# Loading each expert's first weights as 512 pieces of 2 KB in place of 128 pieces of 8 KB

## The reference, cut to what matters

```
logits = xf @ wr + br
topk_vals, topk_idx = jax.lax.top_k(logits, K)          # E = 4 experts, K = 2
h = jax.nn.gelu(jnp.einsum('nd,edh->enh', xf, w1) + b1[:, None, :], approximate=False)
y = jnp.einsum('enh,ehd->end', h, w2) + b2[:, None, :]
```

## Time and profile before

| | |
|---|---|
| Median of 3 runs | 2584.3 us (2577.14 to 2584.51) |
| Profiled execution | 2576.5 us, its span 2574.7 us |
| PE (TensorE) busy | 2089.3 us, 81% of the span |
| DVE, ACT, POOL busy | 1759.0, 1570.7, 1016.1 us |
| DMA | 375.69 MB in 306117 packets, mean 146 GB/s |
| Queue q1 (SP's issues) | 38.6% of 16 engines' span |
| Queue q0 (POOL's) | 8.9% |
| Loads of `moe_w_tile` | 94 of 1024 KB, median 5.3 us from issue to landing |

### The profile page before, as it was taken

The page is one execution under the profiler, slowest core; times in us unless marked ns, Lnnn a source line. Parts: engine busy times, 40 slices in busy tenths (PEclk is TensorE's granted clock), DMA queues, the critical chain, the costliest instruction groups (busy, mean ns, idle before and its releaser), DMA issues. The chain is left out here.

```text
span 2574.7 us, 46905 instructions
## 1 busy us (share of the span) xinstructions
PE 2089.3 (81%) x12000; PEld 1628.2 (63%) x12000; DVE 1759.0 (68%) x7891; ACT 1570.7 (61%) x2744; POOL 1016.1 (39%) x1092
## 2 busy tenths in 40 slices
PE   1344688788888888898898889999888998999965
PEld 1122466676766666676676767777766787777742
DVE  4777667676777777677787778787767554544343
ACT  1034446456666776676677677777666676666542
POOL 1445455545444544344455444444444212111110
PEclk8655699898999999999999899999989999999976
DMA  7354534344445555534555455555554445455431
GB/s 268 98 149 119 172 117 145 111 141 136 127 129 165 170 150 145 170 112 131 150 177 156 141 147 159 175 165 150 143 177 136 142 129 168 136 160 169 150 99 51
DMA packets 306117, 375.69 MB, mean 146 GB/s; under 512 B 127122, under 2 KB 251447, under 8 KB 292924
## 3 DMA queue, kind: packets, MB, share of 16 engines
q1 hardware_dynamic: 274848, 297.02, 38.6%
q0 software_dynamic: 28672, 68.21, 8.9%
q10 hardware_dynamic: 2332, 7.47, 0.7%
HBM read 291.23 MB, written 72.93 MB: 141 GB/s over the span
## 5 line engine op out<-in xcount | busy, mean ns | idle before, releaser
L1204 POOL DMA_INDIRECT w_win<-in_windows,w_idx x512 | 542.0, 1059 | 831.3 <-DMA w_win<-in_windows,w_idx 665.4
L1595 PE MATMUL bank<-moe_w,moe_hidden_T 128*128 x2528 | 640.3, 394 | 13.5 <-DVE moe_y L1037 11.5
L1579 PE MATMUL bank<-moe_xT,moe_w_tile 128*128 128x256 f32 (+1 forms) x3008 | 641.3, 358 | 8.4 <-ACT moe_xT L1364 8.3
L1579 PEld LDWEIGHTS bank<-moe_xT,moe_w_tile 128*128 128x128 f32 x3008 | 517.7, 197 | 85.2 <-ACT moe_xT L1364 14.5
L1595 PEld LDWEIGHTS bank<-moe_w,moe_hidden_T 128*128 128x128 f32 x2528 | 475.6, 197 | 88.8 <-issue 26.7
L818 DVE TENSOR_TENSOR w_prod<-w_win,w_hat 128x36 f32<-128x36 f32 x4096 | 494.3, 218 | 27.2 <-DMA w_win<-in_windows,w_idx 24.1
L1381 ACT ACTIVATE moe_hidden_T<-bank,moe_b 128x256 f32<-128x256 f32 (+1 forms) x752 | 288.8, 437 | 210.7 <-PE bank L1579 207.5
L1238 POOL DMA_INDIRECT moe_y_back<-moe_out_sorted,rows_back x128 | 129.4, 1011 | 275.9 <-DMA moe_y_back<-moe_out_sorted,rows_back 157.3
L1224 POOL DMA_INDIRECT moe_in_sorted<-c,rows x128 | 141.9, 1109 | 236.4 <-DMA moe_in_sorted<-c,rows 100.5
L1381 ACT ACT_TABLE_LOAD x129 | 165.5, 1283 | 72.9 <-PE bank L1579 70.6
L1123 DVE SCALAR_TENSOR_TENSOR hidden_back<-bank,back_stats,hidden_back 128x512 f32<-128x512 f32 x128 | 95.5, 746 | 115.9 <-ACT hidden_back L1421 115.5
(11 more groups left out here) (258 smaller groups left out, 3797.7 us busy)
## 6 DMA issues: line engine op xcount, KB each, us to landing
moe_w_tile<-in_moe_w SPq DMA_DIRECT2D x94, 1024.0 KB, 5.3
L_cond_W<-in_L_cond_W SPq DMA_DIRECT2D x128, 256.0 KB
adapters<-in_adapter SPq DMA_DIRECT2D x128, 192.5 KB
gamma_beta<-in_gamma_beta SPq DMA_DIRECT2D x128, 128.0 KB
moe_x<-moe_in_sorted SPq DMA_DIRECT2D x64, 256.0 KB
moe_out_sorted<-moe_y SPq DMA_DIRECT2D x64, 256.0 KB
x_front<-in_x SPq DMA_DIRECT2D x32, 256.0 KB
w_win<-in_windows,w_idx POOLq DMA_INDIRECT x512
```

The costliest lines, as they stand in the source:

```text
L1204: gp.indirect_dma_start(out=V[:, g_ * WLEN:(g_ + 1) * WLEN], out_offset=None, in_=t["windows"], in_offset=bass.IndirectOffsetOnAxis(ap=idx ...
L1579: last = te.matmul((H0, H1)[r % 2][:, (f % FPU) * TILE:(f % FPU) * TILE + width(n)], W1[n % 3][:, d * F + f * P:d * F + (f + 1) * P], XT[: ...
L1595: last = te.matmul(Y[:, u * D:(u + 1) * D], hT[:, (f % (2 * FPU)) * TILE + u * P:(f % (2 * FPU)) * TILE + (u + 1) * P], ap(moe2, weight + ...
```

## The change

The host lays the experts' first weights out in another order, and the load reads them in that order. Before, each partition's 8 KB (2048 values) of an expert lay in one piece. Now the 2048 values are cut in four parts of 512 values (2 KB, `WPK`); part 0 of all 128 partitions comes first, then part 1, and so on. An expert is then 1 MB in one piece, made of four stretches of 256 KB. The load reads 4 pieces of 2 KB for each partition, 256 KB apart, and puts them in the same places in the buffer as before. The register that holds the plan's offset is used as a row number in an array with 128 values a row, so the same number still points at the expert.

```
+WPK = 512
...
-                sp.dma_start(W1[n % 3][:, :], t["moe_w1"][:, bass.ds(col, NDB * F)]).then_inc(s_w1[n % 3], 16)
+                sp.dma_start(W1[n % 3][:, :].rearrange("p (c f) -> p c f", f=WPK),
+                             t["moe_w1"][bass.ds(col, NDB * F), :].rearrange("(c p k) d -> p c (k d)", p=P, k=WPK // P)
+                             ).then_inc(s_w1[n % 3], 16)
...
-        "moe_w1": np.concatenate([blocks(w) for w in a["L1_ffn_w1"]], 1),
+        "moe_w1": np.concatenate([blocks(w).reshape(P, -1, WPK).transpose(1, 0, 2).reshape(-1, P) for w in a["L1_ffn_w1"]], 0),
```

## The result

The changed kernel takes 2590.02 us in the median of 20 runs (2571.62 to 2607.24), the kernel before 2579.36 us (2562.62 to 2590.18, 20 runs). The ratio is 1.0044, with a 95% interval of 1.0023 to 1.0065: slower by 11 us, where 3 us were forecast. Two later comparisons, each on another chip, gave 1.0087 (1.0052 to 1.0121) and 1.0094 (1.0059 to 1.0128). A ratio here is that of the comparison with its runs; it isn't always the quotient of the two medians (for the last it would be 1.0070).

A forecast was written before the change was run, and what follows sets the result against it. TensorE was taken to bound the stretch of the loads, not the DMA engines. A tenth of POOL's and SP's delays, 2.1 + 1.3 = 3.4 us, on the median 2584.3 gave 2587 us, range 2578 to 2595 (over all cases 2571 to 2603).

The forecast's parts named there:

- Nobody waits for a load: Expert-weight loads: issued about 46 us ahead and landing after 5.3 us, so a load's own speed is worth nothing.
- The transfer itself: DMA engines: a load in 2 KB pieces takes 2.68 us an engine, not 2.47; 20 us more for 94 loads.
- A tenth of the delays reaches the end: POOL and SP delays: 2.1 us of 20 us and 1.3 us of 12 us lengthen the run, 3.4 us together.
- SP's issue: SP issuing a load: 0.47 us for 512 pieces, 0.13 us more a load, 12 us of SP in all.
- The gathers beside a load: POOL's gathers: each waits for the whole load as before, 0.21 us longer, 20 us of POOL's time.
- Rival 1: POOL's gathers get in after 8 pieces, held 0.67 us instead of 2.41; faster, 2567 us; chance 0.12.
- Rival 2: SP's issues behind a load stand until its pieces drain, 1.2 us a load; slower, 2599 us; chance 0.18.
- Rival 3: Load still made in 8 KB packets, or the 0.21 us vanishes in idle DMA time; 2584 us; chance 0.08.

The follow-up runs named there:

- the cut alone: Kernel before with 512 pieces of 2 KB a load, each partition's kept in its own row, 4 KB apart: ratios 1.0007 and 0.9981 against the kernel before.
- The doubled transfer: Kernel before with each load followed by a copy of the same 1 MB into DRAM: 2703.05 against 2574.82 us, ratio 1.0488.
- the finer cut: Kernel before with 2048 pieces of 512 bytes a load, each partition's in its own row, 1 KB apart: 2570.10 against 2581.67 us, ratio 0.9953.
- the order alone: Kernel before with only the DRAM order changed, each expert 1 MB in one piece, still read in 128 pieces of 8 KB: ratio 1.0015.

## Why the prediction was right and where it was wrong

The time fell within the range and moved to the side that the sum gave, and there was luck in it: the sum came out at 3 us for 11 us, and 2590 us lies near 2587 us partly because the kernel before came out at 2579 us over 20 runs, 5 us below the median that the sum started from. Most of the chance, 0.66, lay on a time within 0.3%, and all three comparisons put the change above that (0.44, 0.87 and 0.94%). The third has 2599.72 us, outside the forecast's own 2578 to 2595 us.

- **"Nobody waits for a load":** right. No run shows a wait of TensorE for one.
- **"The transfer itself", 0.21 us more a load:** right as a sum, and by luck. Inside a load the packets take 0.084 us as read (199 packets, 104.7%), but over whole loads they take 0.099 us in the cut alone and 0.104 us in the change, and those of 8 KB 0.388 us and not 0.309 us. A load's packets went from 3.10 to 3.32 us an engine, 0.22 us more, of which the cut is 0.08 us and the order 0.14 us. The prediction gave all of it to the cut; that a partition's pieces now lie 256 KB apart was costed at nothing, and no sentence says so.
- **"A tenth of the delays reaches the end":** this is the step that failed. The order's 13 us of DMA time cost 20 us (2599.72 against 2579.93 us), more than its whole. The doubled transfer's 233 us cost 128 us. The cut's own 8 us cost nothing that can be told (0.9981 and 1.0007), and the finer cut's 49 us came with a gain. There is no one share. The sum also has 2.1 and 1.3 us as tenths of 20 and 12 us, where they are 2.0 and 1.2 us.
- **"SP's issue", 0.13 us:** too much; 0.04 us, and 0.388 us even for 2048 pieces. Some 0.86 us of other work for SP ahead of each load cost nothing at all.
- **"The gathers beside a load" wait for the whole of it:** right. Take the window gathers that are issued with a load (from 0.2 us ahead of it to 1.5 us behind) and for which the next gather waits: in two profiles of the kernel before 42 of 44 had their last packet behind the load's last, and in three of the change 66 of 67. From the load's issue to the next gather it is 5.85 and 5.93 us in the median before, and 6.23, 6.54 and 6.58 us in the change. That they are held longer by more than the 0.21 us is likely and not shown: the order alone has 6.18 us, with no loss.
- **Rival 1 (the gathers get in):** no. POOL's wait for its window gathers didn't fall by 100 us in any kernel: in 300:2450 us it is 626 us with the doubled transfers and 519 to 561 us in all others, where before has 532.6 us. The finer cut is faster, but its 547.3 us of waiting show no such gain, so this rival doesn't explain it.
- **Rival 2 (SP is held up):** not for 512 pieces, where the issues behind a load stay at 0.38 us in the median and under 1 us. For 2048 pieces it came true as a mechanism, 1.13 us in the median and 4.1 us at most, and the kernel was faster and not slower. So the chance of slower, which lay mostly on this rival, was right in its side and not in its reason.
- **Rival 3 (nothing changes):** no; the packets are cut.

The Trainium skill, in "DMA: Bandwidth & Descriptors", section "Latency and other measured facts", has a row on row pitches of large powers of two, for copies between tensors in HBM: they slow down at 2 MiB and more, hardly at 512 KiB, and 4 KiB of padding restores the rate. Here, for loads into SBUF, a distance of 256 KB between a partition's pieces cost 4% of a load's packet time (3.32 against 3.18 us), and 4 KB of padding gave back about half of that (3.24 us). So the remedy agrees in part, and a cost shows at a smaller distance than the row has. Whether the cause is how the memory spreads addresses is open: no run here shows it.

Also open: why more time on SP ahead of a load, or pieces of 512 bytes, makes the whole faster by 0.4 to 0.5%; and how 0.14 us more of packets a load become 0.2 us at the end for each of 94. A part of it is in the matmuls: for the same 12000, TensorE is busy for 2102.0, 2093.9 and 2098.1 us in the three profiles of the change, and 2091.8 and 2091.1 us in the two of the cut alone. In the third comparison the runs' mean granted clock is 0.895 for the change and 0.899 for the cut alone, but it is 0.900 for the change in the first, so a lower clock isn't the whole of it. Whether slower matmuls follow from the longer waits, or make some of the loss themselves, no run here separates.

## What to carry to other kernels

A change of a DMA's shape has two parts, the size of its pieces and their order in DRAM, and each has its price. Try each alone: the cut alone told here what no single packet's duration did. Before a number of a profile counts as an effect, read it in two profiles of the unchanged kernel; the landing times fell by that. Look also at what comes behind the changed transfer, since a longer hold-up there stood in no line of the load itself. And measure once what a delay costs at the end (a doubled transfer does it) before taking a share by feeling, and don't take it for a constant.

## What the runs showed of the hardware

Pieces of 2 KB took 99 ns a packet over whole loads when a partition's lay 4 KB apart, 104 ns when they lay 256 KB apart, and 101 ns with 4 KB of padding between; in a stretch of 1 us inside a load of the change it was 84 ns. A load of 512 or of 2048 pieces took SP 0.388 us in the median to issue, against 0.343 us for one of 128. Behind the load of 2048 pieces SP's next issue took 1.13 us in the median, up to 4.1 us, against 0.38 us behind one of 512. A gather issued with a load got its last packet behind the load's last in 42 of 44 cases when the load was 128 pieces, in 66 of 67 for the change's 512, and in 14 of 18 for 2048.
